# Division of the attention heads in step 1, next rows prepared from group 1 on, last routing and expert weights earlier

## What is computed

```python
def _L0_xattn_ref(x, cond, wq, bq, wkv, bkv, wp, bp):      # 16 heads of 32, 1601 context rows
    q = _qdq(x) @ _qdq(wq).T + bq                          # _qdq: int8 rounding by row
    kv = cond @ wkv.T + bkv
    attn = softmax(einsum('bnhd,bmhd->bhnm', q, k) / sqrt(32))
    o = einsum('bhnm,bmhd->bnhd', attn, v)
    return _qdq(o) @ _qdq(wp).T + bp

def _moe(x, topk_idx, topk_w, w1, w2, w3):                 # 32 experts, 4 chosen per row, 128 slots each
    h = silu(einsum('ech,ehf->ecf', buf, w1)) * einsum('ech,ehf->ecf', buf, w3)
    ob = einsum('ecf,efh->ech', h, w2)

x = x + tanh(g_xattn[0]) * _L0_xattn_ref(_layernorm(x), ctx_2048, ...)
x = x + tanh(g_ffn[0]) * _L0_ffn_ref(_layernorm(x), ...)   # experts and a shared gated FFN of 512
```

## Time and profile before

| | |
|---|---|
| median of 3 runs | 3088.6 us (3077.08 to 3096.61) |
| the profiled execution, time | 3097.04 us |
| its span, first to last instruction | 3095.3 us |
| mean granted clock of PE | 0.959 |
| PE busy | 2759.0 us, 89% of the span |
| DVE busy | 1918.4 us, 62% |
| ACT busy | 1369.7 us, 44% |
| POOL busy | 1809.2 us, 58% |

### The profile page before, as it was taken

The page is one execution under the profiler, slowest core; times in us unless marked ns, Lnnn a source line. Parts: engine busy times, 40 slices in busy tenths (PEclk is TensorE's granted clock), DMA queues, the critical chain, the costliest instruction groups (busy, mean ns, idle before and its releaser), DMA issues.

```text
span 3095.3 us, 42827 instructions
## 1 busy us (share of the span) xinstructions
PE 2759.0 (89%) x14612; PEld 1140.5 (37%) x14652; DVE 1918.4 (62%) x3814; ACT 1369.7 (44%) x2436; POOL 1809.2 (58%) x1558
## 2 busy tenths in 40 slices
PE   5898999899989988989899899989999889997987
PEld 3333333333333333333333333333332334443766
DVE  6577667766776677667767766776676334343222
ACT  4155545654564466455545654564455410110111
POOL 0186667666666685667576757665677432424455
PEclk9799999999999999999999999999999999999999
DMA  3111012101211031103111311220112123232995
GB/s 127 36 51 52 24 35 73 54 22 35 76 52 40 18 91 47 44 13 98 37 35 25 97 27 36 62 65 22 35 49 63 69 89 123 72 112 70 299 292 114
DMA packets 146584, 215.56 MB, mean 70 GB/s; under 512 B 24984, under 2 KB 78232, under 8 KB 146368
## 3 DMA queue, kind: packets, MB, share of 16 engines
q1 hardware_dynamic: 130496, 195.95, 20.9%
q0 software_dynamic: 15872, 16.87, 3.0%
HBM read 126.49 MB, written 34.24 MB: 52 GB/s over the span
## 4 chain that ended last, share of the span: by engine, by line
PE 64%; DVE 14%; ACT 7%; DMA 6%; issue 6%; SPq 2%; POOL 1%; another core or an unknown queue 1%; POOLq 0%; ACTq 0%; DVEq 0%
PE o_ps L873 11%; PE s_ps L859 10%; PE r_all L748 9%; PE r_all L777 8%; PE r_all L787 8%; DVE piece_max L1312 7%; PE r_all L828 6%; DMA out_rows<-probs,slot_init 4%; ACT probs L1096 4%; PE sum_ps L886 3%; PE r_all L846 3%; SPq L555 1%; DVE amax L1166 1%; PE sum_ps L894 1%; POOL prob_acc L1581 1%
## 5 line engine op out<-in xcount | busy, mean ns | idle before, releaser
L1581 POOL TENSOR_TENSOR prob_acc<-prob_acc,probs 128x512 f32<-128x512 f32 x1140 | 1431.9, 1291 | 380.8 <-ACT probs L1096 379.2
L1096 ACT ACTIVATE probs<-s_ps 128x512 f32<-128x512 f32 (+1 forms) x1664 | 936.9, 596 | 762.6 <-PE s_ps L859 736.2
L1312 DVE TENSOR_REDUCE piece_max<-r_all 128x1 f32<-128x400 f32 (+1 forms) x2048 | 1024.9, 565 | 128.2 <-PE r_all L787 123.6
L787 PE MATMUL r_all<-k_flat,q_stack 96*128 96x400 f16 (+1 forms) x2048 | 608.5, 351 | 100.2 <-DVE piece_max L1312 55.1
L859 PE MATMUL s_ps<-q_stack,k_flat 97*128 97x512 f16 (+1 forms) x1664 | 625.8, 395 | 57.4 <-ACT probs L1096 50.6
L873 PE MATMUL o_ps<-probs,v_sb 128*32 128x512 f32 (+1 forms) x3328 | 462.5, 629 | 21.4 <-ACT probs L1096 21.4
L859 PEld LDWEIGHTS s_ps<-q_stack,k_flat 97*128 97x128 f16 (+1 forms) x1664 | 158.1, 100 | 616.0 <-ACT probs L1096 430.0
L1578 POOL COPY prob_acc<-probs 128x512 f32<-128x512 f32 x128 | 73.1, 615 | 501.9 <-PE sum_ps L894 367.1
L787 PEld LDWEIGHTS r_all<-k_flat,q_stack 96*128 96x128 f16 x2048 | 203.1, 100 | 394.5 <-DVE piece_max L1312 202.8
L1613 POOL DMA_INDIRECT slot_rows<-payload,slot x128 | 125.3, 979 | 281.9 <-DVE slot L1490 215.8
L828 PE MATMUL r_all<-probs,k_flat 128*128 128x512 f32 x512 | 223.4, 594 | 2.0 <-DVE sum_sb L1452 1.2
(11 more groups left out here) (220 smaller groups left out, 2714.4 us busy)
## 6 DMA issues: line engine op xcount, KB each, us to landing
k_flat<-k_hi SPq DMA_DIRECT2D x256, 100.1 KB, 2.2
ctx_raw<-in_ctx SPq DMA_DIRECT2D x96, 256.0 KB, 2.9
xin<-in_x SPq DMA_DIRECT2D x16, 1024.0 KB, 5.6
k_flat<-k_lo SPq DMA_DIRECT2D x128, 100.1 KB, 2.2
v_sb<-in_L_ffn_w SPq DMA_DIRECT2D x18, 512.0 KB
q_stack<-q_hi SPq DMA_DIRECT2D x256, 32.0 KB, 1.8
...
```

Source lines behind the costliest of these rows:

```text
L787: last = nc.tensor.matmul(ps[:, 0:w], q_stack[0:KSPLIT, g % 2, j, qt * P:(qt + 1) * P], k_stack[0:KSPLIT, g % 2, j, at:at + w], start=True ...
L1096: nc.scalar.activation(probs[0:w, slot, j, :], s_ps[j % SBANKS][0:w, :], ACT.Exp).then_inc(probs_ready, 1)
L1312: V.reduce_max(piece_max[:, j * TT + qt, i:i + 1], ps[:, 0:PIECE[i]], X_AXIS).then_inc(free_of(*key), 1)
L1581: last = G.tensor_tensor(prob_acc[:, j, :], prob_acc[:, j, :], probs[:, slot, j, :], ALU.add)
```

## The change

Four things change.

1. `divide_heads` moves on DVE from the end of step 0 to the end of step 1, behind the last two key tiles of the group (and, in group 0, a value tile). PE's transpose of the heads stays in step 2 (step 10 in group 1).
2. NEXT_X becomes 6, counted from group 1: the statistics of the next rows stand in group 1, step 7, the square root in step 8, X_RSTD in 9, X_NORM in 10 and 11, X_SCALE in 12, X_ROUND in group 2, steps 0 and 1, X_CLIP in 1 and 2, X_INT in 3 and 4. In `rows_out` x1 is written ahead of h and waits for the statistics of h alone.
3. In batch 6's FFN, hT, logitsT and logits of batch 7 stand between its gate and up tiles; hT of batch 7 has a buffer of its own. DVE routes batch 7 while batch 6's down tiles are made, and its counts stand behind its first two tiles.
4. There are 12 places for expert weights. Experts 7 and 8 are loaded when the last up tile is done, expert 9 when the last down tile is done, into the space of the shared weights. The slot table is loaded from POOL's queue instead of SP's.

```diff
-FIRST_X, NEXT_X = 1, 1
+FIRST_X, NEXT_X = 1, 6
-HOMES, EARLY_HOMES, FREE_HOMES = 9, 7, 5
+HOMES, EARLY_HOMES, FREE_HOMES, GATE_HOMES, DOWN_HOMES = 12, 7, 5, 2, 1
...
+def next_x(g, kt):
+
+    return (g - 1) * KT + kt - NEXT_X
...
 def ffn_tiles(f):
 
     gates = gate_tiles(f)
-    order = gates[0:6] + [("cum", f), ("total", f)] + gates[6:]
+    counts = [("cum", f), ("total", f)]
+    down = [("down", f, t) for t in range(TT)]
+    if f == B - 1:
+        return gates[0:2] + counts + gates[2:] + down
+    if f == B - 2:
+        return (gates[0:2] + [("hT", f + 1, c) for c in range(DC)] + gates[2:3] + [("logitsT", f + 1)] + gates[3:6]
+                + [("logits", f + 1)] + counts + gates[6:] + down)
+    order = gates[0:6] + counts + gates[6:]
...
             def rows_out(b):
 
+                sp.wait_ge(h_var_ready, b + 1)
+                sp.dma_start(x1_v[b], xin[:, :, :]).then_inc(x1_out, DMA)
                 sp.wait_ge(h_ready, (b + 1) * TT)
                 sp.dma_start(h_v[b], work[:, :, :]).then_inc(h_out, DMA)
-                sp.dma_start(x1_v[b], xin[:, :, :]).then_inc(x1_out, DMA)
...
                 if f == B - 1:
-                    sp.wait_ge(slots_written, B * TT * TOPK * DMA)
-                    sp.dma_start(e_slots[:, :, :], slot_v).then_inc(e_slots_in, DMA)
+                    key = ("up", f, FSC - 1)
+                    sp.wait_ge(bank_full[ring.last_bank(*key)], ring.done(*key))
+                    for e in range(EARLY_HOMES, EARLY_HOMES + GATE_HOMES):
+                        expert_weights_in(e)
+                    key = ("down", f, TT - 1)
+                    sp.wait_ge(bank_full[ring.last_bank(*key)], ring.done(*key))
+                    expert_weights_in(EARLY_HOMES + GATE_HOMES)
...
-                    if j == 1 and g == 2 and b + 1 < B and kt == X_STD + NEXT_X:
+                    if j == 1 and g in (1, 2) and b + 1 < B and next_x(g, kt) == X_STD:
                         deviations(x_var_ready, b + 2, x_std_ready)
...
-                if kt == 0 and s:
+                if kt == 1 and s > KT:
                     divide_heads(s // KT - 1)
-                if g == 2 and b + 1 < B:
-                    x_part(b + 1, kt - NEXT_X)
+                if g in (1, 2) and b + 1 < B:
+                    x_part(b + 1, next_x(g, kt))
...
                 for t in range(TT):
+                    if f == B - 2 and t < 3:
+                        routing[t](f + 1)
                     add_shared(f, t)
...
+            G.dma_start(e_slots[:, :, :], slot_v).then_inc(e_slots_in, DMA)
             pool.wait_ge(h_out, B * DMA)
             pool.wait_ge(e_slots_in, DMA)
```

More of the change, by code:

```diff
@@ L171, in ffn_tiles, with logits_after @@
     gates = gate_tiles(f)
-    order = gates[0:6] + [("cum", f), ("total", f)] + gates[6:]
+    counts = [("cum", f), ("total", f)]
[6 more added lines that the diff above has]
+    order = gates[0:6] + counts + gates[6:]
     if f == 0:
         order += [("oiT", B - 1, c) for c in range(DC)] + [("y", B - 1, t) for t in range(TT)]
-    down = [("down", f, t) for t in range(TT)]
-    if f + 1 < B:
-        order += [("hT", f + 1, c) for c in range(DC)] + down[0:1] + [("logitsT", f + 1)]
-        down = down[1:] + [("logits", f + 1)]
-    return order + down
+    order += [("hT", f + 1, c) for c in range(DC)] + down[0:1] + [("logitsT", f + 1)]
+    return order + down[1:] + [("logits", f + 1)]
+def logits_after(f):
+    if f == B - 2:
+        return {("logitsT", f + 1): [0], ("up", f, 1): [1], ("gate", f, 2): [2, 3]}
+    return {("logitsT", f + 1): [0], ("down", f, 1): [1], ("down", f, 2): [2, 3]} if f + 1 < B else {}
 def steps():
@@ L666, in _ @@
             sp.wait_ge(route_ready, B)
-            for e in range(EARLY_HOMES, HOMES):
+            for e in range(EARLY_HOMES + GATE_HOMES + DOWN_HOMES, HOMES):
                 expert_weights_in(e)
@@ L928, in _ @@
                         logits_ps = open_tile(*key)
-                        logits_chunk(logits_ps, f + 1, 0)
-                        continue
-                    tile(key)
-                    if f + 1 < B and key[0] == "down" and key[2] == 1:
-                        logits_chunk(logits_ps, f + 1, 1)
-                    if f + 1 < B and key[0] == "down" and key[2] == 2:
-                        logits_chunk(logits_ps, f + 1, 2)
-                        close(logits_chunk(logits_ps, f + 1, 3), "logitsT", f + 1)
+                    else:
+                        tile(key)
+                    for c in logits_after(f).get(key, []):
+                        last = logits_chunk(logits_ps, f + 1, c)
+                        if c == DC - 1:
+                            close(last, "logitsT", f + 1)
             def rows_transposed(e):
@@ L1068, in tile @@
                     ps = full(act, *key)
-                    nc.scalar.copy(hT[:, key[2], :], ps[:, :]).then_inc(free_of(*key), 1)
+                    nc.scalar.copy(hT[b][:, key[2], :], ps[:, :]).then_inc(free_of(*key), 1)
                 elif kind == "logitsT":
@@ L1496, in _ @@
                 for c in range(FSC):
-                    if f and c < 2:
-                        routing[c](f)
-                    if f and c == 1:
-                        expert_masks(f)
-                    if f and c == 2:
+                    if 0 < f < B - 1:
+                        if c < 2:
+                            routing[c](f)
+                        if c == 1:
+                            expert_masks(f)
+                        if c == 2:
+                            expert_weights(f)
+                    swiglu(f, c)
+                    if f < B - 1 and c == 2:
+                        slots_of_experts(f)
+                    if f == B - 1 and c == 0:
                         expert_weights(f)
-                    swiglu(f, c)
-                    if c == 2:
                         slots_of_experts(f)
```

12 lines of the change are left out of this document (8 added, 4 removed).

## The result

The changed kernel takes 3155.6 us (median of 4 runs, 3147.7 to 3164.4), the kernel before beside it 3090.7: a ratio of 1.0213, 95% interval 1.0194 to 1.0232. It is 2.1% slower; forecast were 1.3% and 3128 us, with a range up to 3158. The profiled execution took 3155.7 us (span 3154.0, mean granted clock 0.952).

A forecast was written before the change was run, and what follows sets the result against it. It took PE, busy nearly nine tenths of the span, as the bound, with DVE pacing parts of groups 1 and 2. Terms summed to +39.8 us on 3097.0, giving 3136.8; less 8.4 to the median, 3128 us, range 3085 to 3158.

The forecast's parts named there:

- the forecast itself: The prediction's main case for the whole kernel, a time between 3108 and 3145 us; chance 0.45.
- groups 3, b0 to 6: Group 3: PE waits 5.4 us at the heads' transposes plus 1.7 for the clock, 7 times; +49.7 us, bounds 38 and 62.
- groups 0: Group 0: the division ends some 0.7 us after the transpose's old place, 7 times; +4.9 us.
- groups 1, b0 to 6: Group 1 takes the next rows' work, 6.2 us each, 7 times; +43.4 us, bounds 28 and 56.
- groups 2, b0 to 6: Group 2 sheds next-rows work, row maximum 6.1 us earlier, clock 1.5 us, 7 times; -53.2 us.
- group 2 of b7: Last batch's group 2 has the wait but no next rows: 5.4 + 0.8 less 1.3; +4.9 us.
- FFN: Batch 6's FFN: PE waits 2 us for h's load, the down phase loses 2.3 us of logits waits; -0.3 us.
- experts: Routed experts at the end start without the 12.4 us wait, then row additions set the pace; -9.6 us, bounds -5 and -16.
- the wait is made up again: Rival: slack in the same group takes back most of each of 15 transpose waits; 3059 us, chance 0.12.
- The block of the next rows moves at no loss: Rival: group 1 +28 instead of +43, group 2 -69 instead of -53; 3097 us, chance 0.25.
- The clock takes more: Rival: two half-clock stretches behind each of 15 waits and each group 1 block; 3153 us, chance 0.18.
- the dear price: Group 2's clips: every pair slowed beside GpSimd's additions, some 0.6 us more per group, 4 us in all.

The follow-up runs named there:

- nx9: div0 with NEXT_X = 9 instead of 6, so the next rows' statistics start in group 1, step 10; 0.9942 of the kernel before.
- end12: nx9 with the next rows' statistics, square root, reciprocal and shift at the end of step 12 of group 1; 0.9874 of the kernel before.
- b_div1: The kernel before with only the heads' division moved to step 1; 1.0243 of the kernel before.
- b_tail: The kernel before with only items 3 and 4 of the change (routing forward, expert weights, slot table's queue); 0.9993 of the kernel before.
- div0: The changed kernel with the heads' division put back in step 0; 0.9978 of the kernel before.
- exp_ahead: end12 plus a one-column exponential on ACT in step 0 of group 2, loading the exponentials' table early; 0.9807 of the kernel before.
- b_next: The kernel before with only item 2 of the change (NEXT_X = 6, x1 written ahead of h); 0.9990 of the kernel before.

## Why the prediction was right, and by how much not

It was right in sign, and in where the time would go: the waits at the transposes, with group 1 paying for what group 2 gains. In size it was lucky: the measured 3155.6 us lies 2.4 us inside the range and outside 3108 to 3145, which it called the forecast itself. Groups 1 and 2 came out 34.1 us dearer than forecast, and groups 0 took back 14.3 of it for a reason that the prediction did not have. Of the 27.6 us between 3128 and 3155.6, 18.9 are the sum (+39.8 forecast, +58.7 between the spans) and the rest is the base: the forecast took off 8.4 us because the profiled execution lay above the median, but the one after lay at its median.

| term, us | forecast | measured |
|---|---|---|
| groups 3, b0 to 6 | +49.7 | +47.3 |
| groups 0 | +4.9 | -9.4 |
| groups 1, b0 to 6 | +43.4 | +64.6 |
| groups 2, b0 to 6 | -53.2 | -40.3 |
| group 2 of b7 | +4.9 | +1.6 |
| groups 1 and 3 of b7 | 0 | -1.1 |
| FFN | -0.3 | +3.3 |
| experts | -9.6 | -7.8 |

- **Groups 3**: 5.4 + 1.7 = 7.1 each; measured 4.92 of waiting and 2.2 of clock (1.5 to 2.5), less 0.3 in step 3. PE waited for the division 23 times, 80.4 us in all: 15 times in groups 2 and 3 (3.49 to 5.25 us), 7 times for 0.2 us in groups 0, and once for 4.28 us behind the last step, where the kernel before waits as long (4.25). The 15 come to 74.6 us; forecast were some 80.
- **Groups 1** is the term that was most mis-sized, 9.2 us each for 6.2 and outside its bounds. The wait for the rows (0.90 for 0.7), the statistics (2.85) and the row scales at nothing came as forecast, the shift even free of charge, at 1161 behind 2.01 us of DVE's own idle time. What failed was "PE then comes out of a wait of over 3 us at the lower clock: 0.9": step 9 took 2.2 us more, mean of seven groups (batch 3: 7.27 for 4.55 at a clock of 0.55, 2.7 us). And the "0.6" for normalising: step 12 took 2.5 us more, mean of seven. Where the clock stayed up, in batch 4, it was those 0.6 (10.83 us for 10.28, with the waits of 0.48 and 0.64 us). In five groups of seven the clock fell a second time, and they took 12.47 or 14.15 us. What brings this second fall is not shown: two groups had such short waits without it, nx9 had it without normalising in group 1. end12, in which PE does not stand in step 8 and normalising is in group 2, is back at 61.1 us.
- **Groups 2**: the step was "two context tiles 1.4, two clips 2.2: 1163.3. From there nine steps of 4.33 us". The nine steps took 39.35 us for 39.7. But DVE stood idle 3.26 us before the first context tile, waiting for the late PE, and began the maxima 8.6 us after the division for 6.5: the row maximum came 62.9 us into the group, 4.3 us earlier than before and not 6.1. The forecast let the engine behind the waiting one run on; its own rival had said that it cannot.
- **Groups 0**: 0.2 us of waiting, as small as thought. The gain is clock: these groups last between 82.1 and 84.6 us in every kernel, by how much of step 4 runs at the lower level (11.2 us on average before, 9.5 after, the idle time in it 2.2 and 2.4). The clock fell there in all seven groups before, behind a wait of 1.97 us for DVE's maxima, and in two of seven after, behind 1.84. Why it falls less often when the division is in step 1 (three of seven in b_div1) stays open.
- **FFN and experts**: the new FFN took 425.8 to 430.2 us in four profiles (changed, b_tail, div0, exp_ahead), the old one 419.2 to 424.9 in three (before, b_div1, b_next). PE waits 1.9 us for the load of h, as forecast (2), and 5.2 us for DVE's additions for 3.2 before, which the forecast had at nothing; the 2.3 us to be gained did not come (see the last section). Additions came every 7.4 us for the first 20 experts, as said. PE's wait for the first rows did not vanish. The slot writes ended 5.2 us before the last down tile and not 9.6; POOL stood 4.39 us ahead of the second of them, for nothing that the profile shows; and from the end of the last write to PE's first matmul it was 13.3 us, 7.4 before. Of these 6.0 us, 2.4 lie ahead of the gather: POOL issues the slot table's load 3.15 us after its last write, where SP had issued it 1.2 us after. By these rows item 4's own change of queue cost some 2 us here; it was not tried alone. The other 3.6 lie between the first gather's issue and PE's matmul (7.25 us for 3.66); the loads of expert 9 and the output rows were issued beside it, from 2913.11 to 2914.62, but that those delayed it was not tried.

The rivals: "the wait is made up again" is refuted by b_div1 (+69 us of attention). "The block of the next rows moves at no loss" failed in both halves: group 1 +64.6 us and not +28, group 2 -40.3 and not -69. "The clock takes more" named 3153 us, nearer to the result than the forecast's own; but half of its 37 us is 18.7 and gives 3147, so the 25 and the nearness are partly an accident. In substance it is half right: groups 3 paid 2.2 us, between its two stretches (3.4) and the forecast's one (1.7), and group 1 paid twice in five batches of seven.

On the clips the dear price was not met. The clips' line in the changed kernel, duration in ns as min/median/max:

```profile
L1263 DVE TENSOR_SCALAR xin<-xin x32: 411/416/1514, 61.9 to 2118.6; 128x512 f32<-128x512 f32 x32
```

Timeline of DVE and POOL, group 2 of batch 3:

```profile
1196.26 0.75 DVE L1263 TENSOR_SCALAR xin<-xin 128x512 f32<-128x512 f32 x2
1203.17 1.83 DVE L1263 TENSOR_SCALAR xin<-xin 128x512 f32<-128x512 f32 x2
...
1193.30 2.48 POOL L1611 TENSOR_TENSOR prob_acc<-prob_acc,probs 128x512 f32<-128x512 f32 x2 [1.33 <-ACT probs L1120]
1200.62 8.01 POOL L1611 TENSOR_TENSOR prob_acc<-prob_acc,probs 128x512 f32<-128x512 f32 x6 [4.84 <-ACT probs L1120]
```

The first pair fell into a gap of POOL and took 0.75 us, the second stood beside additions and took 1.83; the median fell from 1.12 to 0.42 us. The Trainium skill (SBUF — State Buffer, "SBUF: two separate sides") says that the ports which the two engines share go as an exclusive lock to whichever instruction starts first, for its whole length, where VectorE's has two SBUF inputs or runs in a 2-port mode. The multiplication, with two SBUF inputs, took 0.69 or 1.83 us in agreement; so do the clips, if they run in such a mode, which no row shows, as none shows the lock itself.
